# Attention over nodes: three heads through the exponential and then a minimum, one head clipped first

## The reference, cut to what matters

```python
def _L1_gnn_ref(embeds, qW, kW, vW, rows, cols):
    q = (embeds[rows] @ qW).reshape(e, HEADS, dh)
    k = (embeds[cols] @ kW).reshape(e, HEADS, dh)
    v = (embeds[cols] @ vW).reshape(e, HEADS, dh)
    scores = jnp.clip(jnp.einsum('ehd,ehd->eh', q, k), -10.0, 10.0)
    exp_s = jnp.exp(scores)
    norms = jax.ops.segment_sum(exp_s, rows, num_segments=nvar)[rows]
    w = exp_s / (norms + 1e-08)
    res = jax.ops.segment_sum(w[:, :, None] * v, rows, num_segments=nvar).reshape(nvar, d)
    return embeds + res
```

## Time and profile before

| | us |
|---|---|
| median of three runs | 3051.39 |
| lowest, highest | 3047.96, 3053.4 |
| span of the profiled execution | 3063.5 |
| VectorE busy in the span | 2202.0 (72%) |
| TensorE busy | 2495.9 (81%) |
| ScalarE busy | 1221.0 (40%) |
| GpSimd busy | 533.3 (17%) |
| attention's main loop, in the span | 1090 to 1646 |

### The profile page before, as it was taken

The page is one execution under the profiler, slowest core; times in us unless marked ns, Lnnn a source line. Parts: engine busy times, 40 slices in busy tenths (PEclk is TensorE's granted clock), DMA queues, the critical chain, the costliest instruction groups (busy, mean ns, idle before and its releaser), DMA issues. The chain is left out here.

```text
span 3063.5 us, 63275 instructions
## 1 busy us (share of the span) xinstructions
PE 2495.9 (81%) x21713; PEld 1814.2 (59%) x21714; DVE 2202.0 (72%) x4727; ACT 1221.0 (40%) x2285; POOL 533.3 (17%) x936
## 2 busy tenths in 40 slices
PE   4999998999999967777677677787786777777797
PEld 2555555999999821111112366676673666776797
DVE  8999998655656579999998465566564655665645
ACT  2888886333333279999996200000012000000123
POOL 1111110000000010000000433433414334334100
PEclk9999999999999978888987787888787878887798
DMA  2333333110101041111112311111133111111340
GB/s 73 131 128 131 143 138 130 34 34 23 44 23 34 6 120 38 37 37 37 37 38 98 113 48 49 48 49 51 45 56 143 39 53 44 49 51 44 88 194 17
DMA packets 95193, 206.50 MB, mean 67 GB/s; under 512 B 21620, under 2 KB 61172, under 8 KB 94880
## 3 DMA queue, kind: packets, MB, share of 16 engines
q1 hardware_dynamic: 80544, 182.38, 17.0%
q0 software_dynamic: 14464, 21.44, 3.8%
HBM read 118.17 MB, written 84.76 MB: 66 GB/s over the span
## 5 line engine op out<-in xcount | busy, mean ns | idle before, releaser
L1804 PE MATMUL l_bank<-tab,mask 128*128 128x192 f16 x7600 | 796.4, 265 | 291.4 <-issue 280.4
L1804 PEld LDWEIGHTS l_bank<-tab,mask 128*128 128x128 f16 x7600 | 694.0, 105 | 389.8 <-issue 377.2
L1395 DVE TENSOR_SCALAR mask<-code 128x1600 int32<-128x1600 int32 x304 | 540.9, 1813 | 468.2 <-remote 393.3
L1776 POOL DMA_INDIRECT ggot<-table_dram,gidx x432 | 411.9, 953 | 148.5 <-issue 123.9
L1277 DVE SCALAR_TENSOR_TENSOR pr<-ex,cring 128x1568 f32<-128x1568 f32 x200 | 355.8, 1779 | 14.9 <-DMA cring<-c_dram 10.3
L1204 PE MATMUL score<-qa,ka 96*128 (+1 forms) x800 | 229.4, 386 | 146.4 <-DVE least L1270 130.0
L1204 PEld LDWEIGHTS score<-qa,ka 96*128 96x128 f16 x800 | 54.1, 103 | 380.8 <-DVE least L1270 185.3
L816 PE MATMUL sums<-onehots,ct 128*128 128x192 f16 x3125 | 265.9, 249 | 13.8 <-issue 5.3
L816 PEld LDWEIGHTS sums<-onehots,ct 128*128 128x128 f16 x3125 | 262.2, 99 | 17.3 <-issue 10.9
L816 PE MATMUL sums<-u,ct 128*128 128x192 f16 x3125 | 259.1, 246 | 0.0
L816 PEld LDWEIGHTS sums<-u,ct 128*128 128x128 f16 x3125 | 258.0, 98 | 0.0
(11 more groups left out here) (341 smaller groups left out, 2828.7 us busy)
## 6 DMA issues: line engine op xcount, KB each, us to landing
code<-code_dram SPq DMA_DIRECT2D x38, 800.0 KB, 4.3
code_dram<-flat SPq DMA_DIRECT2D x100, 200.0 KB, 1.9
ct_dram<-ct SPq DMA_DIRECT2D x25, 800.0 KB, 3.6
c_dram<-flat SPq DMA_DIRECT2D x25, 800.0 KB, 3.3
ct_again<-ct_dram SPq DMA_DIRECT2D x25, 800.0 KB, 16.8
cring<-c_dram SPq DMA_DIRECT2D x200, 98.0 KB, 1.9
table_dram<-tab SPq DMA_DIRECT2D x50, 384.0 KB, 2.3
flat<-code_dram SPq DMA_DIRECT2D x19, 800.0 KB, 4.3
```

Source lines behind the costliest of these rows:

```text
L1395: e.tensor_scalar(turned.rearrange("p (s q d) -> p s q d", q=NQ, d=DQ // 2), words.rearrange("p (q s d) -> p s q d", q=NQ, d=DQ // 2), abs ...
L1776: e.indirect_dma_start(ggot[:, k, j, :], None, table_dram[:, :], bass.IndirectOffsetOnAxis(ap=gidx[:, k, j:j + 1], axis=0)).then_inc(s_ggo ...
L1804: mm = e.matmul(acc[k][:, 0:2 * D], mask[:, r % MR, s, :], tab[:, s, r, :], start=(r == 0 and s == 0), stop=(r == R - 1 and s == NT - 1))
```

## The change

The first head alone now keeps the clip in front of the exponential, on ScalarE. The scores of the other three heads go from PSUM straight into one exponential on ScalarE (which takes on the multiplication by `poss`), into `ex`. VectorE then takes the minimum of these with exp(10), in place; since the exponential rises, this is the same bound as a clip of the score at 10. VectorE's own clip and the ring `least` are gone, and `short` is half as wide. The PSUM banks are dealt out anew: one for the first head, two sets of three for the others (used by tiles in turn), and one for the sums, as before. ScalarE's loop now runs over all eight blocks, with this order in a tile: clip of the first head, exponential of the three, exponential of the first. VectorE's order keeps its form: minimum of tile j+1, masking of tile j.

```diff
--- before.py
+++ after.py
@@ -54,6 +54,7 @@
 SLOTS = 3
 NCHG = -(-NCH // GG) * GG
 EXP_LOW = math.exp(-10.0)
+EXP_HIGH = math.exp(10.0)
 
 
 class Chain:
@@ -1154,17 +1155,17 @@
             with ExitStack() as main:
                 sb = new_sb(main)
                 UR = 5
-                short = [sb(f"short{k}", [P, 2, QC], F32) for k in range(UR)]
-                least = [sb(f"least{k}", [P, 2, QC], F32) for k in range(UR)]
+                short = [sb(f"short{k}", [P, QC], F32) for k in range(UR)]
                 ex = [sb(f"ex{k}", [P, H, QC], F32) for k in range(UR)]
                 pr = [sb(f"pr{k}", [P, H, QC], F32) for k in range(UR)]
                 ten = sb("ten", [P, 1], F32)
                 poss = sb("poss", [P, 1], F32)
-                sc_ps = [main.enter_context(nc.psum_tensor(f"score{k}", [P, 2, 512], F32)) for k in range(2)]
+                first_ps = main.enter_context(nc.psum_tensor("score_first", [P, 512], F32))
+                rest_ps = [main.enter_context(nc.psum_tensor(f"score_rest{k}", [P, H - 1, 512], F32)) for k in range(2)]
                 acc = main.enter_context(nc.psum_tensor("att_acc", [P, 512], F32))
-                s_sc = [sem(f"l1_score{k}") for k in range(2)]
-                s_short, s_least, s_ex, s_pr, s_pv, s_acc, s_ten, s_pad = (sem("l1_" + k) for k in
-                                                                           ("short", "least", "ex", "pr", "pv", "acc", "ten", "pad"))
+                s_sc = [sem("l1_score_first"), sem("l1_score_rest")]
+                s_short, s_rest, s_ex, s_capped, s_pr, s_pv, s_acc, s_ten, s_pad = (
+                    sem("l1_" + k) for k in ("short", "rest", "ex", "capped", "pr", "pv", "acc", "ten", "pad"))
                 s_bd, s_bd_in = sem("l1_bd"), sem("l1_bd_in")
                 AHEAD = 3
                 with nc.Block() as block:
@@ -1196,14 +1197,14 @@
                         def scores(b, j):
                             if j in first_keys:
                                 e.wait_ge(s_spread[first_keys.index(j)], SPREAD)
-                            for pair in range(2):
-
-                                e.wait_ge((s_short, s_least)[pair], b * NT + (j + 1))
-                                for o in range(2):
-                                    h = 2 * pair + o
-                                    mm = e.matmul(sc_ps[pair][:, o, 0:QC], ka[0:D, h, j * P:(j + 1) * P],
-                                                  qa[0:D, h, bass.ds(b * QC, QC)], start=True, stop=True)
-                                mm.then_inc(s_sc[pair], 1)
+                            key = lambda h: ka[0:D, h, j * P:(j + 1) * P]
+                            query = lambda h: qa[0:D, h, bass.ds(b * QC, QC)]
+                            e.wait_ge(s_short, b * NT + (j + 1))
+                            e.matmul(first_ps[:, 0:QC], key(0), query(0), start=True, stop=True).then_inc(s_sc[0], 1)
+                            e.wait_ge(s_rest, b * NT + (j + 2 if j == 0 else j + 1))
+                            for h in range(1, H):
+                                mm = e.matmul(rest_ps[j % 2][:, h - 1, 0:QC], key(h), query(h), start=True, stop=True)
+                            mm.then_inc(s_sc[1], 1)
 
                         def sums(b, j):
                             e.wait_ge(s_pr, b * NT + (j + 1 + UR))
@@ -1232,47 +1233,37 @@
 
                     @block.scalar
                     def _(e):
-                        def clip(b, j):
-
+                        def tile(b, j):
                             e.wait_ge(s_sc[0], b * NT + (j + 1))
-                            e.activation(short[j % UR][:], sc_ps[0][:, :, 0:QC], ACT.Relu, bias=ten[:],
+                            e.activation(short[j % UR][:], first_ps[:, 0:QC], ACT.Relu, bias=ten[:],
                                          scale=negs[:]).then_inc(s_short, 1)
-
-                        def exp(b, j, pair):
-                            e.wait_ge((s_short, s_least)[pair], b * NT + (j + 2))
-                            if pair == 0:
-                                e.wait_ge(s_pr, b * NT + (j + 1))
-                                e.activation(ex[j % UR][:, 0:2, :], short[j % UR][:], ACT.Exp, bias=ten[:], scale=-1.0)
-                            else:
-                                e.activation(ex[j % UR][:, 2:4, :], least[j % UR][:], ACT.Exp).then_inc(s_ex, 1)
-
-                        def blk(b, last):
+                            e.wait_ge(s_sc[1], b * NT + (j + 1))
+                            e.wait_ge(s_pr, b * NT + (j + 1))
+                            e.activation(ex[j % UR][:, 1:H, :], rest_ps[j % 2][:, :, 0:QC], ACT.Exp,
+                                         scale=poss[:]).then_inc(s_rest, 1)
+                            e.wait_ge(s_short, b * NT + (j + 2))
+                            e.activation(ex[j % UR][:, 0, :], short[j % UR][:], ACT.Exp, bias=ten[:],
+                                         scale=-1.0).then_inc(s_ex, 1)
+
+                        e.sem_inc(s_short, 1)
+                        e.sem_inc(s_rest, 2)
+                        e.wait_ge(s_ten, 2)
+                        with e.Fori(0, NQB) as b:
                             for j in range(NT):
-                                exp(b, j, 0)
-                                if j + 1 < NT:
-                                    clip(b, j + 1)
-                                elif not last:
-                                    clip(b + 1, 0)
-                                exp(b, j, 1)
-
-                        e.sem_inc(s_short, 1)
-                        e.wait_ge(s_ten, 1)
-                        clip(0, 0)
-                        with e.Fori(0, NQB - 1) as b:
-                            blk(b, False)
-                        blk(NQB - 1, True)
+                                tile(b, j)
 
                     @block.vector
                     def _(e):
-                        def clip(b, j):
-
-                            e.wait_ge(s_sc[1], b * NT + (j + 1))
-                            e.tensor_scalar(least[j % UR][:], sc_ps[1][:, :, 0:QC], poss[:], 10.0,
-                                            ALU.mult, ALU.min).then_inc(s_least, 1)
+                        def capped(b, j):
+
+                            e.wait_ge(s_rest, b * NT + (j + 3))
+                            e.tensor_scalar(ex[j % UR][:, 1:H, :], ex[j % UR][:, 1:H, :], EXP_HIGH, None,
+                                            ALU.min).then_inc(s_capped, 1)
 
                         def masked(b, j):
                             e.wait_ge(s_c[j % CR], b * (16 * (NT // CR)) + 16 * (j // CR + 1))
                             e.wait_ge(s_ex, b * NT + (j + 1))
+                            e.wait_ge(s_capped, b * NT + (j + 1))
                             e.wait_ge(s_pv, b * NT + (j + 1))
                             e.scalar_tensor_tensor(pr[j % UR][:], ex[j % UR][:], EXP_LOW,
                                                    cring[:, j % CR, :].unsqueeze(1).to_broadcast([P, H, QC]),
@@ -1286,9 +1277,9 @@
                         def blk(b, first, last):
                             for j in range(NT):
                                 if j + 1 < NT:
-                                    clip(b, j + 1)
+                                    capped(b, j + 1)
                                 elif not last:
-                                    clip(b + 1, 0)
+                                    capped(b + 1, 0)
                                 masked(b, j)
                                 if first and j == NT - 1:
                                     e.wait_ge(s_bd_in, 16 * LOADS)
@@ -1303,9 +1294,8 @@
                         e.sem_inc(s_pr, UR)
                         e.sem_inc(s_pv, UR)
                         e.sem_inc(s_acc, 1)
-                        e.sem_inc(s_least, 1)
                         e.wait_ge(s_ten, 2)
-                        clip(0, 0)
+                        capped(0, 0)
                         blk(0, True, False)
                         with e.Fori(1, NQB - 1) as b:
                             blk(b, False, False)
@@ -1927,8 +1917,6 @@
                                     if t or r >= MR:
                                         masked(t, r)
                                     if t == 1 and r >= MR:
-                                        if r == MR:
-                                            e.wait_ge(s_used, n + 1)
                                         rest_added(r - MR)
                                     if r == MR and t > 1:
                                         summed(t - 1)
```

## The result

The changed kernel takes 2993.8 us (median of four runs, 2989.5 to 2997.1) against 3049.7 (four runs, 3044.9 to 3053.4): ratio 0.9817, 95% interval 0.9803 to 0.9831. That is 56 us less. I had forecast 40 less and 3011 us, with a range from 2998: right in sign and in where the gain comes from, but one term of the sum was wrong, and the time lies 4 us outside the range.

The account below looks back on a forecast made before the run. VectorE was taken as the bound, busy 517.50 of the stretch's 522 us. Best case 469 us plus 40% of the 32 us to the worst gave 482, 40 less: 3051.4 - 40 = 3011 us, range 2998 to 3028.

Parts of the forecast that it names:

- VectorE's part: VectorE in the attention's tiles: a minimum of 778 ns replaces the 1025 ns clip, pitch 2.39 us, 0.25 less.
- best case: The 194-tile stretch if VectorE never waits: 469 us, 53 less than 522.
- ScalarE's part: ScalarE's three activations a tile take 675, 1234 and 619 ns, 2.23 us after overlaps against 2.48.
- the wait at the head of a block: TensorE's longer wait at tile 0 of a block for the score banks tile 24 used: cost 0, at most 2 us.
- the loop: Masking, sums, scores, exponential and minimum close after three tiles: 6.6 us at high clock, 7.2 at low; does not bind.
- The sum: Stretch time put 40% of the way from best case, 469 us, to worst, 501: 482 us, 40 less.
- After the stage nothing changes: Code behind the attention stage keeps its time; a granted clock that falls a little may move some 3 us.
- if by more than 53, something outside the two engines' sums was bound: Sign to check: how a move of the stage's end by more than 53 us was to be read.
- TensorE as the bound: Rival: TensorE at its low clock bounds the stretch, only 21 us less, 3030 us; chance 0.12.
- One element a step: Rival: VectorE's minimum runs at one element a cycle, 1368 ns, pitch 2.98 us, 3117 us; chance 0.04.
- Low clock throughout: Rival: TensorE stays at its low level, 2.88 us a tile, 42 us more, 3093 us; chance 0.02.
- Order: Rival: the minimum ahead of masking waits for ScalarE, so the old pitch stays, 3049 us; chance 0.06.

Follow-up runs that it names:

- second execution: The changed kernel without an edit on a second chip: 2567.4 us against 2626.9 for the kernel before there, ratio 0.9773; stretch 468.0 us.
- 9: Changed kernel with scores issued two tiles in front of the sums instead of three: stretch 656.6 us, 3.38 us a tile.
- Experiment 3: Changed kernel plus one more VectorE minimum of 392 unused elements a tile: stretch 518.8 us, ratio 0.9983 to the kernel before.
- Experiment 1: Kernel before with only VectorE's wait for the last gather turn in the next layer removed: ratio 0.9999 to the kernel before, stretch 524.5 us.
- 4: Changed kernel without VectorE's minimum: stretch 439.4 us, 2.26 us a tile, ratio 0.9673 to the kernel before.
- 8: Changed kernel with the minimum out of place, from one dense run into three separate rows: minimum 1373 ns, stretch 582.3 us, ratio 1.0215 to the kernel before.

## Why the prediction was wrong

- **VectorE's part: right.** 0.26 us a tile where I had 0.25; the pitch is 2.38. My best case of 468.8 us for the stretch was in effect what came: 466.2, and 468.0 in the second execution.
- **ScalarE's part, the wait at the head of a block, the loop: right.** Each duration within 1.5%, and with one tile less ahead the loop showed at the computed size (9).
- **The sum: this step failed.** "With less slack I take 40% of the way" added 13 us to the best case. By my own working 9 of these were waits for TensorE at its low clock and 4 the table loads (8 x 1.3 = 10 of the 32 us between the cases). Measured is 0.1 us of idle time, and 1.5 in the second execution; I had expected VectorE's busy share to fall to 97%, and it is 100%. The term is 13 of the 17 us by which I missed; 2.6 more are the better pitch, and 1.7 is the kernel before, whose median over four runs is 3049.7 and not 3051.4. Two things were wrong in it. First, I kept the 28% of low clock of the earlier trace rows as if it were a property of the stage. It depends on the pace: at 2.38 us it was 6% (0.97) and 12% (0.94). VectorE's shorter work closes up TensorE's tiles, and the table shows the clock rise with it. With 6% in place of 28% my sum would have put 2 us in place of the 9. Second, I spread the low clock evenly over the tiles and took a share of its whole cost. In the changed kernel's stretch it comes in a few spells of three tiles at most, and little or nothing of their cost reached VectorE. The timeline of the changed kernel (start us, us, engine, line, operation, in brackets the idle time before it) shows one of the longest, behind the copy at the end of a block:

```profile
1173.34 0.55 DVE L1275 COPY flat<-att_acc 128x392 f32 x1
...
1173.95 1.54 PE L1214 MATMUL att_acc<-pr,v 128*32 128x392 f32 x8 [2.14 <-DVE flat L1275]
...
1175.96 0.68 ACT L1238 ACTIVATE short<-score_first,ten,negs 128x392 f32<-128x392 f32 x1 [1.57 <-PE score_first L1203]
...
1176.20 0.75 DVE L1260 TENSOR_SCALAR ex<-ex 128x1176 f32<-128x1176 f32 x1
...
1176.83 1.54 PE L1214 MATMUL att_acc<-pr,v 128*32 128x392 f32 x8
...
1178.58 0.75 DVE L1260 TENSOR_SCALAR ex<-ex 128x1176 f32<-128x1176 f32 x1
...
1178.85 0.68 ACT L1238 ACTIVATE short<-score_first,ten,negs 128x392 f32<-128x392 f32 x1 [0.16 <-PE score_first L1203]
...
1179.72 0.87 PE L1214 MATMUL att_acc<-pr,v 128*32 128x392 f32 x8
...
1181.10 0.78 DVE L1260 TENSOR_SCALAR ex<-ex 128x1176 f32<-128x1176 f32 x1
```

  TensorE's sums take 1.54 us (the low level) from 1173.95 on, 0.87 from 1179.72 on; its tiles come 2.88 us apart. ScalarE waits 1.57 us for the first scores. But VectorE's minimums stand at 1176.20, 1178.58 and 1181.10: 2.38 and then 2.52 us. It lost 0.14 us, on the third tile. As an estimate, each further tile at the low level would have cost half a microsecond (2.88 less 2.38). Experiment 3 is the strongest case by number, 38% low and no idle time on VectorE, but at 2.66 us a low tile lags only by 0.2. At 2.38 the second execution shows the limit: 12% low, and 1.5 us of idle time.
- **After the stage nothing changes: true, but not by my argument.** I had not read the diff's last hunk, a removed wait in the next layer. Experiment 1 finds it worth 0 (within 0.1%), on the chip where that layer is shorter. An unread hunk is a term of the sum without bounds.
- **The range.** Its low end, 2998, was the best case itself. That the best case has an uncertainty of its own (21 ns of the minimum are 4 us over 194 tiles, the median of before another 2) was left out on that side. For the same reason its sign "if by more than 53, something outside the two engines' sums was bound" misleads: the stage gave 55.8, and the rest was VectorE's own pitch.
- **The rivals.** TensorE as the bound: refuted by 4, where it and ScalarE supply a tile every 2.26 us. One element a step: real where the shapes are unlike (8), absent here. Low clock throughout: it is two ahead that brings it near (9), not this change. Order: refuted by the window above.

## What to carry to other kernels

Where one engine is busy without a gap and the others work two or three tiles ahead, price a change by that engine's pitch and by the idle time that it has left, and ask of each disturbance whether it lasts longer than the store of finished tiles, not how often it comes. A granted clock read from the trace of before is itself a result of the pace, and moves when the pace does. And look at the shape of both sides of a one-source VectorE instruction before its element count: here, dense on both sides took 757 ns and dense into separate rows 1373.

## What the runs showed of the hardware that I had not expected

The same kernel takes 3050 us on one chip and 2628 on another. The stretch is nearly the same (522 and 524 us). The difference lies in the relations' layer, whose code is written out without a loop. There TensorE's matmul of a node's features with the masks, L1804, waited for nothing that the profile shows ("issue"), first in the kernel before on the first chip, then in experiment 1's kernel on the second:

```profile
L1804 PE MATMUL l_bank<-tab,mask x7600: 242/246/368, 1719.3 to 2886.8; 128*128 128x192 f16 x195
...
  issue: 657.6, 742
```

```profile
L1804 PE MATMUL l_bank<-tab,mask x7600: 243/246/368, 1723.2 to 2450.0; 128*128 128x192 f16 x195
...
  issue: 8.1, 2
```

From the first to the last of its 7600 matmuls it takes 1167.5 us on one and 726.8 on the other, 441 us less, and the two profiled spans differ by 437. The idle time of 657.6 us became 8.1 (280.4 of it stood before matmuls and 377.2 before weight loads, which overlap), with a median matmul of the same 246 ns; VectorE's L1395 lost 393.3 us of waiting for a remote cause and has no wait of that kind on the second chip. What differs between the two chips was not tried and stays open. A per cent is therefore not the same on both: the change's 56 and 59.5 us are 1.8% on one and 2.3% on the other.
